# The last block of an eight-stage transformer kernel: which engine empties PSUM, and how many chunks VectorE may lie behind TensorE

## The chip, the cores and the metric

The kernel runs on one core of a Trainium2 chip. The metric is the device time of one execution in microseconds (us), before the change the median of 3 runs. The engines are called PE (TensorE), DVE (VectorE), ACT (ScalarE), POOL (GpSimd) and SP (the queue that issues DMAs).

## The reference

The input x is (4, 512, 256). Eight sublayers follow one another, each `x = x + f(layernorm(x))`: causal attention, a gated feed-forward with retrieved experts, attention over features, the feed-forward again, attention with rotary positions, and then the three that the last block of the kernel computes:

```python
def ffn(x):                              # used twice, before and after the scan, same weights
    h = silu(x @ w_gate) * (x @ w_up)    # 1024 hidden members
    keep the 2 largest magnitudes in each group of 4 members of h, zero the others
    return h @ w_down

def scan(x):
    ct = concat([x shifted by one position, x])
    xv = sigmoid(relu(ct @ W_act.T))     # pairs (re, im) of 128 complex channels
    mag = sqrt(re*re + im*im); m = cummax(mag over positions)
    re, im = re / m, im / m
    kv = cumulative complex product over the 512 positions
    r = sigmoid(relu(ct @ W_rec.T))
    return (kv @ W_val.T) * r**4

x = x + ffn(layernorm(x)); x = x + scan(layernorm(x)); x = x + ffn(layernorm(x))
```

## The kernel before

x stays in SBUF for the whole kernel, as 16 tiles of 128 positions by 256, four tiles (NT) to a batch element. The change touches one function, `feed_forward_and_scan` (from L1438), which computes the last three sublayers for all four batch elements. It has one instruction stream for each engine, and the order of the work is written out by hand.

A **pass** is one feed-forward of one batch element (512 positions): passes 0 to 3 are the first feed-forward of elements 0 to 3, passes 4 to 7 the second. A pass has 8 **chunks** of 128 hidden members (FC = 8), so there are 64 chunks. Every engine walks through the same **slots** n = 0, 1, 2, ... In slot n:

- PE does `chunk(n)`: 6 matmuls for the gate (L1618) and 6 for the up projection (L1624), each a product of high and low halves, into two PSUM banks that chunks n and n+1 use in turn. Then `down(n - 7)` (L1634), 8 records of an fp32 matmul into banks 4 and 5, where a pass sums up, and then the jobs of its list `pe_at[n]`.
- ACT does the silu of the gate's bank (L1724), then `magnitude(n - 1)` (L1712), the absolute value of the product before, then `act_at[n]`.
- DVE does `product(n)` (L1870), silu times the up bank, which it reads from PSUM. Four chunks (a quad) hold the four members of each group, and the quad before is selected in three parts in slots n with n % 4 = 0, 1, 2: comparisons (L1879), counts (L1885 to L1889), and h times the mask (L1894). Then `dve_at[n]`.
- POOL has no slot work of its own; it normalises rows (L1744) when told to, and at the start it makes the low halves of the weights (L1750).

Between engines, semaphores count: a product waits for silu and up, silu(n) for product(n - 2), `down` of a quad for its selection, the first `down` of a pass for the addition of the pass before to x (L1904, DVE, from PSUM), a pass's first chunk for the low halves of its rows (L1763, DVE, from PSUM).

The scan of element b is cut into jobs that start at slot `scan_from(b)` = 8(b+1) + 7, that is 15, 23, 31, 39, and are spread over 16 slots (s is its first): statistics on DVE and normalisation on POOL in s; row transposes in s+2 (L1565); the act gate in s+3 and s+4 (L1574, with tanh and square on ACT, L1674 and L1675); sum of squares s+5; root on ACT s+6 (L1679); running maximum and reciprocal s+6 (L1793, L1794); division and 7 levels s+7, s+8; 6 tree steps s+9, s+10 (each four operations, L1811 to L1815); fill s+11; the output matmul, which waits until the scan is filled, and its two DVE steps for each half in s+12 (L1593, L1840, L1843); statistics of the second feed-forward's rows s+13, their transposes and halves s+15. The gate `rec` (L1583) is in s+6 and s+8. Two scans overlap: s+8 of one is s of the next. Banks 6 and 7 are taken in turn by the jobs that need one (`Turns`, L1427); each bank is free again when the job's own reader has read it.

```python
            for n in range(SLOTS):
                p = (n - DOWN_LAG) // FC - 1
                if (n - DOWN_LAG) % FC == 0 and 0 <= p < PASSES:
                    add_to_x(p)
                if n < CHUNKS:
                    product(n)
                q, part = n // QUAD - 1, n % QUAD
                if 0 <= q < CHUNKS // QUAD and part < 3:
                    select(q, part)
                ...
                for job in dve_at[n]:
                    do(job)
```

## Time and profile before

| | us |
|---|---|
| median of 3 runs (1680.29, 1680.30, 1686.45) | 1680.3 |
| the profiled execution's own time | 1688.6 |
| its span, first to last instruction | 1686.8 |
| the last block's matmuls begin | 1229.5 |
| PE / DVE / ACT / POOL busy in the span | 1423.4 / 1078.2 / 617.3 / 286.1 |
| mean granted TensorE clock | 0.90 |

All times in the rows are counted from the first instruction of the profiled execution. Busy time is time in which an engine's unit works; instructions of DVE that follow one another overlap a little, so start-to-start distances are shorter than the durations. Matmul records of fp32 operands come in twos. A bracket such as `[5.40 <-ACT tail_silu L1724]` is the engine's idle time before the instruction and what ended it.

### The profile page before, as it was taken

Reading aid. Unit: us, or ns where it says so; the run is one execution under the profiler, and the core shown is the slowest. Engines: PE = TensorE matmul, PEld = TensorE weight load, DVE = VectorE, ACT = ScalarE, POOL = GpSimd, SP = SyncE. Lnnn points to the kernel's source line nnn. Section 1 sums busy time; section 2 is a strip of 40 time slices with the busy share of each in tenths; the row PEclk is TensorE's granted clock in tenths of the full one; section 3 lists DMA queues with packets and bytes.
Section 4 is the critical chain, followed back from the end, with each engine's and each line's share of the span. In section 5 each row is a group of like instructions: output and inputs, shape, how many; then the busy total and the mean of one; then the engine's idle time right before and its main releaser. Section 6 shows DMA issues by size and latency. Waiting matters only on the chain. (4 is left out here: it accounts for less than half of the span.)

```text
span 1686.8 us, 21695 instructions
## 1 busy us (share of the span) xinstructions
PE 1423.4 (84%) x8144; PEld 1010.8 (60%) x8144; DVE 1078.2 (64%) x2161; ACT 617.3 (37%) x1144; POOL 286.1 (17%) x239
## 2 busy tenths in 40 slices
PE   3899999858999678799957899988579977979698
PEld 2555555447888567688843334433268765766576
DVE  5555444087788348777647465566367688787875
ACT  1354444343333214333322465566422422333221
POOL 1210000053433102233323030200210101011000
PEclk9799987579999898899976599999979998989899
DMA  6713500040000000000022330300000000000000
GB/s 145 102 28 57 75 3 2 1 145 1 1 1 1 1 1 1 1 1 1 1 54 39 75 66 17 48 2 1 1 1 1 1 0 1 1 1 0 13 13 25
DMA packets 21407, 39.07 MB, mean 23 GB/s; under 512 B 4480, under 2 KB 6272, under 8 KB 21176
## 3 DMA queue, kind: packets, MB, share of 16 engines
q1 hardware_dynamic: 21304, 37.70, 11.9%
q8 instruction: 64, 1.05, 0.3%
q14 instruction: 39, 0.32, 0.1%
HBM read 14.54 MB, written 2.10 MB: 10 GB/s over the span
## 5 line engine op out<-in xcount | busy, mean ns | idle before, releaser
L1274 DVE TENSOR_REDUCE attn_negm<-ps 128x2 f32<-128x1024 f32 (+3 forms) x256 | 256.3, 1021 | 122.9 <-PE ps L903 61.2
L1123 ACT ACTIVATE attn_probs<-ps 128x512 f32<-128x512 f32 (+3 forms) x512 | 236.9, 515 | 211.1 <-PE ps L936 123.5
L453 POOL TENSOR_TENSOR moe_h_low<-moe_h,moe_h_high 128x512 fp32r<-128x512 f32 x96 | 139.7, 1458 | 326.9 <-ACT moe_h_high L403 326.9
L927 PE MATMUL ps<-attn_qs,attn_ks 49*128 49x512 f32 (+4 forms) x512 | 159.5, 437 | 36.6 <-ACT attn_probs L1123 34.5
L1634 PE MATMUL ps<-sb_f_down,tail_h 128*128 128x256 f32 x512 | 132.0, 406 | 56.7 <-DVE x L1904 41.1
L1634 PEld LDWEIGHTS ps<-sb_f_down,tail_h 128*128 128x128 f32 x512 | 102.5, 203 | 78.3 <-DVE x L1904 44.0
L903 PE MATMUL ps<-attn_ks,attn_qs 48*128 48x512 f32 (+4 forms) x512 | 126.4, 490 | 24.7 <-DMA attn_ks<-attn_part_low 18.2
L420 ACT ACTIVATE moe_silu<-ps 128x512 f32<-128x512 f32 x96 | 57.4, 598 | 228.7 <-PE ps L326 228.6
L927 PEld LDWEIGHTS ps<-attn_qs,attn_ks 51*128 51x128 f32 (+1 forms) x512 | 75.8, 204 | 100.9 <-ACT attn_probs L1123 96.1
L951 PE MATMUL ps<-attn_probs,attn_va 128*32 128x512 f32 (+3 forms) x1024 | 132.4, 595 | 0.0
L903 PEld LDWEIGHTS ps<-attn_ks,attn_qs 50*128 50x128 f32 (+1 forms) x512 | 54.4, 209 | 95.6 <-issue 63.8
L1870 DVE TENSOR_TENSOR tail_h<-tail_silu,ps 128x512 f32<-128x512 f32 x64 | 43.8, 686 | 84.5 <-PE ps L1624 45.1
L1724 ACT ACTIVATE tail_silu<-ps 128x512 f32<-128x512 f32 x64 | 38.1, 595 | 114.6 <-PE ps L1618 114.5
L476 DVE TENSOR_TENSOR moe_h<-moe_silu,ps 128x512 f32<-128x512 f32 x64 | 43.4, 687 | 55.2 <-PE ps L333 37.6
L355 PE MATMUL ps<-f_down_high,moe_h_high 128*128 128x256 f32 x256 | 74.3, 290 | 3.7 <-POOL moe_h_low L453 3.7
L355 PE MATMUL ps<-f_down_high,moe_h_low 128*128 128x256 f32 x256 | 72.8, 284 | 0.0
L355 PE MATMUL ps<-f_down_low,moe_h_high 128*128 128x256 f32 x256 | 72.4, 283 | 0.0
L403 ACT ACTIVATE moe_h_high<-moe_h 128x512 fp32r<-128x512 f32 x96 | 60.0, 625 | 27.0 <-DVE moe_h L476 26.4
L1239 DVE RECIPROCAL attn_rden<-ps 128x16 f32<-128x16 f32 x32 | 8.2, 258 | 95.5 <-PE ps L965 95.5
L1618 PE MATMUL ps<-tail_xh,tail_gate_high 128*128 128x512 f32 x128 | 63.0, 492 | 1.4 <-DVE tail_xl L1763 1.4
L1879 DVE TENSOR_TENSOR tail_ge<-tail_mag 128x1536 bf16<-128x1536 f32 (+2 forms) x48 | 55.8, 1219 | 0.7 <-ACT tail_mag L1712 0.7
L936 PE MATMUL ps<-sb_a_mask_kq,sb_identb 64*128 64x128 bf16 x512 | 55.6, 236 | 0.0
(316 smaller groups left out, 3287.1 us busy)
## 6 DMA issues: line engine op xcount, KB each, us to landing
attn_qs<-attn_part_high SPq DMA_DIRECT2D x64, 128.0 KB, 4.8
attn_qs<-attn_part_low SPq DMA_DIRECT2D x32, 128.0 KB, 4.5
attn_ks<-attn_part_high SPq DMA_DIRECT2D x32, 128.0 KB, 5.8
attn_ks<-attn_part_low SPq DMA_DIRECT2D x16, 128.0 KB, 6.6
out_x<-x SPq DMA_DIRECT2D x4, 512.0 KB, 2.8
x<-in_x SPq DMA_DIRECT2D x1, 1536.0 KB, 11.8
attn_qs<-attn_mT SPq DMA_DIRECT2D x64, 4.0 KB
moe_raw<-in_f_gate SPq DMA_DIRECT2D x2, 512.0 KB, 6.1
```

The lines of the kernel that those rows point to most:

```text
L355: last = pe.matmul(ps[:, bank + t // 2, (t % 2) * D:(t % 2 + 1) * D], hp[:, j % RING, t * P:(t + 1) * P], wp[:, jw, :], start=j == 0 and t ...
L403: act.activation(hc.high[:, n % RING, :], h[:, n % RING, :], ACT.Copy).then_inc(high_done, 1)
L420: act.activation(sg[:, j % 2, :], ps[:, 2 * (j % 2), :], ACT.Silu).then_inc(silu_done, 1)
L453: pool.tensor_tensor(hc.low[:, j % RING, :], h[:, j % RING, :], hc.high[:, j % RING, :], ALU.subtract).then_inc(low_done, 1)
L903: last = pe.matmul(ps[:, 2 * (n % 2) + k, 0:width1(qt)], qs[e:e + ROWS1, b % 2, hd // 2, qt * P:(qt + 1) * P], ks[e:e + ROWS1, b % 2, key_ ...
L927: last = pe.matmul(ps[:, SC + k, 0:width2(kt)], ks[e:e + ROWS2, b % 2, key_tile(hd), kt * P:(kt + 1) * P], qs[e:e + ROWS2, b % 2, hd // 2, ...
L951: last = pe.matmul(ps[SLOT * j:SLOT * (j + 1), CTX, T - width2(kt):T], va[:, b % 2, kt, hd % KH, :], pr[:, s3 % RING, j, 0:width2(kt)], st ...
L1123: act.activation(pr[:, s2 % RING, j, 0:n], ps[:, SC + k, 0:n], ACT.Exp, scale=HD ** -0.5).then_inc(exp_done, 1)
L1274: dve.tensor_reduce(m, ps[:, 2 * half:2 * half + 2, 0:width1(qt)], AX, ALU.max, negate=True).then_inc(r1_free, 1)
L1618: last = pe.matmul(ps[:, bank, :], wp[:, c, j * P:(j + 1) * P], xp[:, p % 2, c, :], start=c == 0 and k == 0, stop=c == DC - 1 and k == 2)
L1634: last = pe.matmul(ps[:, DOWN + t // 2, (t % 2) * D:(t % 2 + 1) * D], h[:, j, t * P:(t + 1) * P], w_down[:, j, :], start=j == 0 and t % 2 ...
L1879: c.do(dve.tensor_tensor(ge[:, first:first + n, :], mag[:, lo, :].unsqueeze(1).broadcast_to([P, n, T]), mag[:, lo + 1:4, :], ALU.is_ge))
```

## The change

All in `feed_forward_and_scan`:

- ACT copies the up bank to SBUF (`up`, a ring of 4), so `product` has both operands in SBUF; silu's ring grows from 2 to 4, h from 8 to 12 chunks, the magnitudes from one quad to two. ACT also copies the pass's sum (`dsum`), the scan's output (into `ta`), and the rows of a pass in fp32 (`xf`) beside their high halves. DVE reads no PSUM any more.
- `magnitude` is made 3 slots after its chunk instead of 1, and stands ahead of the up copy. The selection of a quad starts in slot 4q+5 instead of 4q+4, and `down` lies 10 slots behind instead of 7.
- The scan of element b starts at slot 8(b+2) (16, 24, 32, 40) instead of 8(b+1)+7, with its pieces at other distances: all levels and the division in one slot (s+8), the tree in one (s+9), the fill in s+10, DVE's output steps and the statistics after them in s+11, while PE's and ACT's part of the output stays in s+12.
- The low halves of rows are made by POOL in one instruction of 128x1024 for a pass; for pass 0 by DVE. POOL waits for the first normalised rows before it splits the weights.
- The addition to x is one instruction, in slot 8(p+2).

```diff
-    DOWN_LAG = 7
+    RING = 4
+    HRING = 3 * QUAD
+    ABS_LAG, SELECT_LAG, DOWN_LAG = 3, 5, 10
     SLOTS = CHUNKS + DOWN_LAG + 2
     DOWN = 4
     S1 = 8
@@ -1454,64 +1456,68 @@
     TREE = [1 << k for k in range((NS - 1).bit_length())]
 
     def scan_from(b):
-        return FC * (b + 1) + DOWN_LAG
+        return FC * (b + 2)
...
+    def rows_of(p, n):
+        pe_at[n] += [("row", "f", p, c) for c in range(DC)]
+        act_at[n] += [("row", "f", p, c) for c in range(DC)]
+        pool_at[n] += [("low", p)]
+
     for p in range(1, B):
-        pe_at[FC * p - 4] += [("row", "f", p, c) for c in range(DC)]
-        act_at[FC * p - 4] += [("row", "f", p, c) for c in range(DC)]
-        dve_at[FC * p - 4] += [("row", "f", p, c) for c in range(DC)]
-        pool_at[FC * p - 6].append(("normalise", "f", p))
+        pool_at[FC * p - 7].append(("normalise", "f", p))
+        rows_of(p, FC * p - 4)
     dve_at[0].append(("stats", "rest"))
+    for p in range(PASSES):
+        act_at[FC * (p + 1) - 1 + DOWN_LAG].append(("sum", p))
+        dve_at[FC * (p + 2)].append(("add", p))
     for b in range(B):
         s = scan_from(b)
         dve_at[s].append(("stats", "s", b))
-        pool_at[s].append(("normalise", "s", b))
-        pe_at[s + 2] += [("row", "s", b, c) for c in range(DC)]
-        act_at[s + 2] += [("row", "s", b, c) for c in range(DC)]
-        pe_at[s + 3].append(("act", b, 0))
-        pe_at[s + 4].append(("act", b, 1))
-        act_at[s + 3].append(("act", b, 0))
-        act_at[s + 4] += [("act", b, 1), ("square", b)]
+        pool_at[s + 2].append(("normalise", "s", b))
+        pe_at[s + 4] += [("row", "s", b, c) for c in range(DC)]
+        act_at[s + 4] += [("row", "s", b, c) for c in range(DC)]
+        pe_at[s + 5] += [("act", b, 0), ("act", b, 1)]
+        act_at[s + 5] += [("act", b, 0), ("act", b, 1), ("square", b)]
         dve_at[s + 5].append(("sum", b))
-        act_at[s + 6].append(("root", b))
-        dve_at[s + 6].append(("peak", b))
-        dve_at[s + 7] += [("divide", b)] + [("level", b, i) for i in (1, 2, 3)]
-        dve_at[s + 8] += [("level", b, i) for i in (4, 5, 6, 7)]
-        dve_at[s + 9] += [("tree", b, d) for d in TREE[:3]]
-        dve_at[s + 10] += [("tree", b, d) for d in TREE[3:]]
-        dve_at[s + 11].append(("fill", b))
-        pe_at[s + 6].append(("rec", b, 0))
-        act_at[s + 6].append(("rec", b, 0))
-        pe_at[s + 8].append(("rec", b, 1))
-        act_at[s + 8].append(("rec", b, 1))
+        pe_at[s + 7].append(("rec", b, 0))
+        act_at[s + 7].append(("rec", b, 0))
+        act_at[s + 8].append(("root", b))
+        dve_at[s + 7].append(("peak", b))
+        dve_at[s + 8] += [("divide", b)] + [("level", b, i) for i in range(1, S1)]
+        pe_at[s + 9].append(("rec", b, 1))
+        act_at[s + 9].append(("rec", b, 1))
+        dve_at[s + 9] += [("tree", b, d) for d in TREE]
+        dve_at[s + 10].append(("fill", b))
         pe_at[s + 12] += [("out", b, m) for m in range(2)]
-        dve_at[s + 12] += [("out", b, m) for m in range(2)]
-        dve_at[s + 13].append(("stats", "f", B + b))
-        pool_at[s + 13].append(("normalise", "f", B + b))
-        pe_at[s + 15] += [("row", "f", B + b, c) for c in range(DC)]
-        act_at[s + 15] += [("row", "f", B + b, c) for c in range(DC)]
-        dve_at[s + 15] += [("row", "f", B + b, c) for c in range(DC)]
+        act_at[s + 12] += [("out", b, m) for m in range(2)]
+        dve_at[s + 11] += [("out", b, m) for m in range(2)]
+        dve_at[s + 11].append(("stats", "f", B + b))
+        pool_at[s + 14].append(("normalise", "f", B + b))
+        rows_of(B + b, s + 15)
...
-            jobs.take(job, "dve" if job[0] == "out" or job[:2] == ("row", "f") else "act")
+            jobs.take(job, "act")
...
-        sg = s.sb("silu", [P, 2, T])
-        h = s.sb("h", [P, FC, T])
+        h = s.sb("h", [P, HRING, T])
-        mag = s.sb("mag", [P, QUAD, T])
+        mag = s.sb("mag", [P, 2, QUAD, T])
+        xf = s.sb("xf", [P, DC, T])
+        sg, up = s.sb("silu", [P, RING, T]), s.sb("up", [P, RING, T])
+        dsum = s.sb("dsum", [P, 2, T])
...
-                    pe.wait_ge(free["dve"], jobs.count[("row", "f", p, DC - 1)])
+                    pe.wait_ge(xl_ready, p + 1)
...
-                at_least(pe, prod_done, n - 1)
+                at_least(pe, up_done, n - 1)
...
-                    at_least(pe, x_done, p)
+                    at_least(pe, sum_done, p)
...
                 if kind == "f":
-                    act.activation(xT.high[:, k % 2, c, :], ps[:, jobs.bank[job], :], ACT.Copy).then_inc(xh_ready, 1)
+                    at_least(act, xl_ready, k)
+                    act.activation(xf[:, c, :], ps[:, jobs.bank[job], :], ACT.Copy).then_inc(xf_ready, 1)
+                    act.activation(xT.high[:, k % 2, c, :], ps[:, jobs.bank[job], :], ACT.Copy).then_inc(free["act"], 1)
...
+            def values(b, m):
+                job = ("out", b, m)
+                act.wait_ge(ready, jobs.number[job])
+                act.activation(ta[:, m, :], ps[:, jobs.bank[job], :], ACT.Copy).then_inc(free["act"], 1)
+
+            def down_sum(p):
+                act.wait_ge(down_done, FC * (p + 1))
+                at_least(act, x_done, p)
+                act.activation(dsum[:, :, :], ps[:, DOWN:DOWN + 2, :], ACT.Copy).then_inc(sum_done, 1)
...
             def magnitude(n):
                 act.wait_ge(prod_done, n + 1)
                 if n % QUAD == 0:
-                    at_least(act, ge_done, n // QUAD)
-                act.activation(mag[:, n % QUAD, :], h[:, n % FC, :], ACT.Abs).then_inc(mag_done, 1)
+                    at_least(act, ge_done, n // QUAD - 1)
+                act.activation(mag[:, n // QUAD % 2, n % QUAD, :], h[:, n % HRING, :], ACT.Abs).then_inc(mag_done, 1)
...
                 if n < CHUNKS:
                     act.wait_ge(gate_ready, n + 1)
-                    at_least(act, prod_done, n - 1)
-                    act.activation(sg[:, n % 2, :], ps[:, 2 * (n % 2), :], ACT.Silu).then_inc(silu_done, 1)
-                if 1 <= n <= CHUNKS:
-                    magnitude(n - 1)
+                    at_least(act, prod_done, n - RING + 1)
+                    act.activation(sg[:, n % RING, :], ps[:, 2 * (n % 2), :], ACT.Silu).then_inc(silu_done, 1)
+                if 0 <= n - ABS_LAG < CHUNKS:
+                    magnitude(n - ABS_LAG)
+                if n < CHUNKS:
+                    act.wait_ge(up_ready, n + 1)
+                    act.activation(up[:, n % RING, :], ps[:, 2 * (n % 2) + 1, :], ACT.Copy).then_inc(up_done, 1)
                 for job in act_at[n]:
                     do(job)
...
+            def low(p):
+                pool.wait_ge(xf_ready, DC * (p + 1))
+                pool.wait_ge(free["act"], jobs.count[("row", "f", p, DC - 1)])
+                pool.tensor_tensor(xT.low[:, p % 2, :, :], xf[:, :, :], xT.high[:, p % 2, :, :], ALU.subtract).then_inc(xl_ready, 1)
+
+            pool.wait_ge(xn_ready["f"], 1)
             for k, (n, at) in enumerate(parts):
                 pool.wait_ge(w_high, k + 1)
                 pool.tensor_tensor(halves[n].low[at], raw[n][at], halves[n].high[at], ALU.subtract).then_inc(w_low, 1)
             for n in range(SLOTS):
                 for job in pool_at[n]:
-                    normalise(*job[1:])
+                    if job[0] == "normalise":
+                        normalise(*job[1:])
+                    else:
+                        low(*job[1:])
 
         @block.vector
         def _(dve):
             c = Chain(dve, sel_steps, 11)
...
+            def low0():
+                dve.wait_ge(free["act"], jobs.count[("row", "f", 0, DC - 1)])
+                dve.tensor_tensor(xT.low[:, 0, :, :], xf[:, :, :], xT.high[:, 0, :, :], ALU.subtract).then_inc(xl_ready, 1)
...
-                dve.wait_ge(ready, jobs.number[job])
-                dve.tensor_tensor(r4[:, m, :], ps[:, jobs.bank[job], :], r4[:, m, :], ALU.mult).then_inc(free["dve"], 1)
-                dve.wait_ge(free["dve"], jobs.count[job])
+                dve.wait_ge(free["act"], jobs.count[job])
+                co.step(dve.tensor_tensor(r4[:, m, :], ta[:, m, :], r4[:, m, :], ALU.mult))
                 xb = x[:, NT * b + 2 * m:NT * b + 2 * m + 2, :]
                 dve.tensor_tensor(xb, xb, r4[:, m, :].rearrange("p (t d) -> p t d", t=2), ALU.add).then_inc(x_scanned, 1)
...
             def product(n):
-                dve.wait_ge(silu_done, n + 1)
-                dve.wait_ge(up_ready, n + 1)
-                at_least(dve, down_done, n - FC + 1)
-                dve.tensor_tensor(h[:, n % FC, :], sg[:, n % 2, :], ps[:, 2 * (n % 2) + 1, :], ALU.mult).then_inc(prod_done, 1)
+                dve.wait_ge(up_done, n + 1)
+                at_least(dve, down_done, n - HRING + 1)
+                dve.tensor_tensor(h[:, n % HRING, :], sg[:, n % RING, :], up[:, n % RING, :], ALU.mult).then_inc(prod_done, 1)
...
             def add_to_x(p):
-                dve.wait_ge(down_done, FC * (p + 1))
-                for k in range(2):
-                    t0 = NT * (p % B) + 2 * k
-                    xk = x[:, t0:t0 + 2, :]
-                    last = dve.tensor_tensor(xk, xk, ps[:, DOWN + k, :].rearrange("p (t d) -> p t d", t=2), ALU.add)
-                last.then_inc(x_done, 1)
+                dve.wait_ge(sum_done, p + 1)
+                xb = x[:, NT * (p % B):NT * (p % B + 1), :]
+                dve.tensor_tensor(xb, xb, dsum[:, :, :].rearrange("p k (t d) -> p (k t) d", t=2), ALU.add).then_inc(x_done, 1)
...
-            for job in early:
-                do(job)
+            low0()
             for n in range(SLOTS):
-                p = (n - DOWN_LAG) // FC - 1
-                if (n - DOWN_LAG) % FC == 0 and 0 <= p < PASSES:
-                    add_to_x(p)
                 if n < CHUNKS:
                     product(n)
-                q, part = n // QUAD - 1, n % QUAD
+                q, part = (n - SELECT_LAG) // QUAD, (n - SELECT_LAG) % QUAD
                 if 0 <= q < CHUNKS // QUAD and part < 3:
                     select(q, part)
                 if n == FC:
```

## Rows read from the trace of the kernel before

**Rows 1.** Windows: us, busy us (instructions) by engine, granted clock (PEclk), DMA share, GB/s.

```profile
1229.45:1264.30 34.85, 29.59 (x113) 23.63 (x113) 21.89 (x58) 10.36 (x18) 7.18 (x8) 0.84 0.00 1
1264.30:1302.75 38.45, 38.12 (x170) 31.84 (x169) 25.68 (x39) 10.14 (x18) 0.00 (x0) 0.97 0.00 1
1433.89:1505.52 71.63, 57.75 (x243) 45.11 (x241) 59.03 (x141) 22.29 (x32) 6.57 (x8) 0.93 0.00 1
1498.00:1502.00 4.00, 3.58 (x9) 2.86 (x10) 3.83 (x13) 0.00 (x0) 0.00 (x0) 0.50 0.00 0
```

**Rows 2.** Waits, last block: who waited for whom, us, times, longest.

```profile
PE ps L1634 <- DVE x L1904: 41.1, 7, 11.1
```

**Rows 3.** Timeline, DVE: start, us, line, operation, [idle before <- releaser].

```profile
1388.05 0.69 DVE L1870 TENSOR_TENSOR tail_h<-tail_silu,ps 128x512 f32<-128x512 f32 x1 [0.25 <-DVE tail_zz L1815]
...
1438.76 0.69 DVE L1870 TENSOR_TENSOR tail_h<-tail_silu,ps 128x512 f32<-128x512 f32 x1 [2.26 <-PE ps L1634]
1439.37 3.49 DVE L1879 TENSOR_TENSOR tail_ge<-tail_mag 128x1536 bf16<-128x1536 f32 x3
...
1447.21 0.69 DVE L1885 TENSOR_TENSOR tail_count<-tail_ge 128x1024 bf16<-128x1024 bf16 x1
...
1453.43 2.49 DVE L1894 SCALAR_TENSOR_TENSOR tail_h<-tail_count,tail_h 128x512 f32<-128x512 bf16 x4
...
1459.57 0.69 DVE L1870 TENSOR_TENSOR tail_h<-tail_silu,ps 128x512 f32<-128x512 f32 x1 [0.25 <-DVE tail_zz L1815]
...
1470.07 0.69 DVE L1870 TENSOR_TENSOR tail_h<-tail_silu,ps 128x512 f32<-128x512 f32 x1 [5.40 <-ACT tail_silu L1724]
...
1474.38 1.40 DVE L174 BATCH_NORM_STATS2 tail_nf_stats<-x 128x6 f32<-128x256 f32 x4 [0.21 <-DVE tail_ge L1879]
...
1478.80 0.68 DVE L1787 TENSOR_TENSOR tail_sq<-tail_sq 128x512 f32<-128x512 f32 x1
```

**Rows 4.** Chain that ended last, scan round of 1531: start, us, what.

```profile
1531.19 3.69 PE ps L1593 x16
1534.88 3.44 PE ps L1574 x8
1538.32 1.38 PE ps L1618 x6
...
1541.06 1.73 PE ps L1634 x8
```

**Rows 5.** Timeline, PE: three starts after idle time.

```profile
1261.08 3.78 PE L1634 MATMUL ps<-sb_f_down,tail_h 128*128 128x256 f32 x8 [2.96 <-DVEq L1897]
...
1599.37 3.78 PE L1634 MATMUL ps<-sb_f_down,tail_h 128*128 128x256 f32 x8 [5.68 <-DVEq L1897]
1602.94 4.61 PE L1593 MATMUL ps<-sb_s_val,tail_zz 128*128 128x256 f32 x16
```

**Rows 6.** Timeline, ACT, same pass as rows 3.

```profile
1468.40 1.15 ACT L1675 ACTIVATE tail_sq<-tail_z,tail_halfone 128x1024 f32<-128x1024 f32 x1
...
1474.96 1.28 ACT L1679 ACT_TABLE_LOAD   x1
```

**Rows 7.** Timeline, POOL: two normalisations of four tiles.

```profile
1436.60 2.16 POOL L1744 TENSOR_SCALAR tail_xns<-x,tail_minus_s,tail_ns_rstd 128x256 f32<-128x256 f32 x4 [24.77 <-DVE tail_minus_s L1783]
1478.99 4.41 POOL L1744 TENSOR_SCALAR tail_xnf<-x,tail_minus_f,tail_nf_rstd 128x256 f32<-128x256 f32 x4 [40.23 <-DVE tail_minus_f L1783]
```

**Rows 8.** Timeline, POOL and DVE, start of the last block.

```profile
1220.61 2.34 POOL L1750 TENSOR_TENSOR tail_up_low<-sb_f_up,tail_up_high 128x1024 fp32r<-128x1024 f32 x1
1220.71 2.25 DVE L183 TENSOR_TENSOR tail_n_newton<-tail_n_rstd 128x4 f32<-128x4 f32 x1
...
1240.06 0.17 DVE L180 TENSOR_SCALAR tail_n_half<-tail_n_var 128x12 int32<-128x12 int32 x1
```

**Rows 9.** Groups of instructions, last block: busy us, mean ns, idle before.

```profile
L1840 DVE TENSOR_TENSOR tail_r<-ps,tail_r 128x512 f32<-128x512 f32 x8 | 5.5, 692 | 7.3 <-PE ps L1593 7.3
L1843 DVE TENSOR_TENSOR x<-x,tail_r 128x512 f32<-128x512 f32 x8 | 5.5, 691 | 0.3
```

More of the change, by code:

```diff
@@ L1698, in do @@
                     row(*a)
+                elif kind == "sum":
+                    down_sum(*a)
+                elif kind == "out":
+                    values(*a)
                 elif kind == "act":
@@ L1798, in divide @@
                 if b > 0:
-                    dve.wait_ge(ready, jobs.number[("out", b - 1, 1)])
+                    dve.wait_ge(free["act"], jobs.count[("out", b - 1, 1)])
                 dve.scalar_tensor_tensor(zz[:, :, :], z[:, :, :], 1.0, sq[:, 1, :].unsqueeze(1).broadcast_to([P, 2, T]),
@@ L1846, in do @@
                 kind, *a = job
-                if kind == "row":
-                    row(*a)
+                if kind == "add":
+                    add_to_x(*a)
                 elif kind == "stats":
```

20 lines of the change are left out of this document (8 added, 12 removed).

## The prediction

> **What bounds the kernel now.** I read the windows by pass first, then who waited for whom, then one pass instruction by instruction. The change touches only the last block, whose PE work starts at 1229.45 us [rows 1]. Call F the moment when VectorE (DVE) has signalled that a scan is filled; the four of them fall at 1387.9, 1459.4, 1531.1 and 1602.8 us [rows 3 to 5], so one pass with a scan in it takes 71.6 us. A plain pass (slots 8 to 15) takes 38.5 us and TensorE (PE) is busy for 38.1 of them: PE bounds it. In a pass with a scan PE is busy 57.8 of 71.6 us and DVE 59.0 [rows 1]. DVE issues nearly all the time: the waits of that pass longer than 0.2 us add up to 9.7 (2.3, 1.3, 0.2, 5.4, 0.3, 0.2; the two long ones stand in [rows 3]), so 61.9 us is its own work with the small gaps between dependent steps. PE in turn loses 41.1 us in seven waits for the addition to x [rows 2]. So a scan pass is a loop through all engines: DVE's work plus what DVE waits for.
>
> **The change, part by part.** The profiled execution spans 1686.8 us (1688.6 with what lies around it) against a median of 1680.3; I work in the span and carry the difference over.
>
> *Operands from SBUF.* The 64 products and the scan's outputs lose their PSUM operand. An addition that read PSUM took 692 ns and one that read SBUF alone 691 [rows 9]: zero gain by instruction. The Trainium skill (VectorE: DVE Perf Modes, section on the TRN2 errata) gives 58 cycles plus the elements for an SBUF source against 120 for PSUM; by that some 11 instructions a pass would each save 65 ns, an estimate of 5 us in the block. The rows show none of it.
>
> *Work taken from DVE.* The two lows of rows (xl, 0.69 each as any 128x512 operation here) go to GpSimd (POOL), and two additions to x become one: 61.9 - 1.4 leaves 60.5 us of DVE per scan pass. If nothing else waited, that would be the pass. ACT gains 8 copies of 0.6, a copy of the sum and two more copies of rows, some 8 us on an engine busy for 22 of 71.6: hidden, except where a copy stands in a hand-off.
>
> *The start.* POOL now waits for the first normalised rows before it splits the weights. Today its four 2.34 us subtractions hold up four tiny DVE steps (2.25 us each but the first, 1.5, where such a step else takes 0.17) [rows 8]: 7.5 us for the four. The rows come at 1218.5, but two weight subtractions must now follow (1223.2), then DVE's low beside POOL, so chunk 0 starts at 1224.6, 4.9 earlier. Then the longer lags: today chunk 8 starts 34.9 us after chunk 0 (at 1264.3), because slot 7 already holds a down product that waits for the selection. Later it is 8 chunks of 2.72, rows of 0.8 and 1.7 for a cold start, 24.3: chunk 8 at 1249.0. Slots 8 and 9 are chunk alone, slots 10 to 15 chunk and down (2.75 + 1.72 = 4.5) [rows 4]: chunk 16 at 1282.1 instead of 1302.8. Of these 20.7 us, 5.2 are three down products that only come later. The first scan now starts at slot 16, not 15, and its sum waits for ACT's slot 17, so DVE has the statistics at 1298 and the first scan's act gates end at 1318.7 on PE. From there it goes as in the next paragraph, 2.4 us shorter, as no rows cross there: first F at 1374.5, **13.4 earlier**.
>
> *A scan pass, from F (t = 0).* With s the slot in which a scan starts, PE stands at the scan's output of slot s+4 and has idled for about 18 us. After an idle of 11 us the granted clock was 0.50 for 4 us [rows 1], the level of 1.2 GHz. After one of 5.7 us, 8 records of down took 3.8 us instead of 1.7 and the 16 of the output 4.6 instead of 3.7 [rows 4, 5]; I call that cold. So the output takes 5.6, ACT's copy 0.75, DVE's last two steps 1.4: out ends at 7.8, the statistics (4.4, [rows 3]) at 12.2, two products at 13.4. The comparison of slot s+5 needs the magnitude of chunk s+3, which ACT makes in slot s+6, behind the act gates. PE: output 5.6, rows 1.3 (its banks wait for ACT), chunk and down 4.5, both act parts 6.4 (3.2 each, 3.44 with the end of the last matmul [rows 4]) = 17.8. ACT: relu 0.8, tanh and square 2.2 (the square 1.15 [rows 6]), silu and magnitude 1.2 = 22.0. **DVE stalls 8.6 us.** Then comparison 3.6, sum 0.6, product 0.6, counts 2.65, product 0.6, selection 2.6 [rows 3] = 32.7. The peak of slot s+7 needs the root of ACT's slot s+8, behind chunk s+8: PE 17.8 + 8.9 + 0.8 = 27.5, ACT's four copies 2.2, POOL's subtraction 2.9, chunk and its copy 3.7, table load 1.3 [rows 6], root 0.65 = 38.1. **DVE stalls 5.4 more.** What is left of the 60.5 (less the 22.4 already spent) is 38.1, with no wait in it: the next F at 76.2, **4.6 later than today's 71.6**. That holds for two rounds. In the third no new scan starts, which saves its statistics (4.4): 71.8 against 71.7. The moved scan pieces cost nothing by themselves; where they land decides, and both waits are of an earlier DVE slot on a later ACT slot.
>
> *POOL's subtraction.* No row has it. The nearest, 128x1024 of weights, takes 2.34 [rows 8]; POOL's normalisation took 2.16 alone and 4.41 beside DVE [rows 7]. Ends: 2.35 and 4.8. I take 2.9, nearer the lower one, because DVE is about to stall then. The rows also show DVE standing through a POOL instruction. The Trainium skill (SBUF — State Buffer, section "SBUF: two separate sides") says the port pair is an exclusive lock held for the whole instruction, against a GpSimd operation also for a DVE operation with two SBUF inputs, as the products now are. The trace agrees, and that speaks against this edit; rival B has its price.
>
> *The end.* From the last F: chunk 56 waits in the same way for rows, copies and subtraction and starts at 24.8, PE idle for 4.6 before it and so cold (1.9). Chunk 63 starts 31.3 later, at 58.0; its last 2.75 and three downs 5.2 give 66.0; sum, copy and addition 2.6, comparison to selection 9.0, four downs 7.2, copy and addition 2.6, store and rest 3.5 = 90.9. Today 84.0 passes from the last F to the end: **6.9 later**.
>
> Sum: -13.4 + 4.6 + 4.6 + 0.1 + 6.9 = **+2.8 us**, or 1683 at the median. A measurement of this kernel can tell about 0.5% (8.4 us) from no change: below 1671.9 is faster, above 1688.7 slower.
>
> **Rivals.**
> A, the lags do what they say: DVE works through the scans with at most one of the two stalls. Without the stall at the root each of three rounds loses 5.4: 1683 - 16 = 1667; without both, 1641. For it: POOL and ACT are idle for most of the time, and the lags are written for this. Against it: both waits follow from the slot numbers. It decides if the root is through by t = 35. Chance 0.18.
> B, slower: the hand-off at the end of a pass. Rows, four copies and one subtraction now lie in a row before the next chunk. If POOL takes 4.8 beside DVE instead of 2.9, PE idles over 3 us there, and after idles of 3.0 and 5.7 us the next 8 records took 3.8 us [rows 5]. That is 1.9 + 1.3 at three boundaries and 1.9 at the last: +11.5, 1694. It decides from 1.5 us more per boundary. Chance 0.20.
> C, several small waits that I left out, each under 0.3 us, in some 60 slots: +7 to +12, 1690 to 1695. Chance 0.07.
> D, the start gains nothing, since the weights are only split later: +5 to +13, 1688 to 1696. Against it: the 3 us wait before the first down goes in any case. Chance 0.03.
>
> **How the numbers follow.** My forecast (within 5 us of 1683) has 0.52. All of it and part of A's mild end and of B fall within 0.5%: same 0.55. Slower takes most of B, C and D: 0.26; faster most of A: 0.19. The bounds: subtraction at 2.35 (-2), PE not cold at the output (-2 in each round, -6), subtraction at 4.8 (+8), cold boundaries (+4). With A's 1667 and B's 1694 the range is 1667 to 1695; it leaves out A without any stall and the worst of B and C.
>
> **What would show it.** Right: chunk 16 starts near 1282 and the first F at 1374 to 1376; in each scan round DVE waits some 8 us for a magnitude and some 5 for the root; the distance between two F is 76; the clock is at half when the output starts; the last F is at 1598 to 1600. Wrong: a distance below 71, PE busy when the scan is filled, or a comparison that doesn't wait; on the other side POOL's subtraction above 4 us, or PE idle for more than 3 us at the boundary. If chunk 0 isn't earlier than 1227, the start is misjudged.

## The result and the profile after

The changed kernel takes **1696.4 us**, the median of 20 runs (1685.6 to 1716.6). The kernel before takes 1684.4 in 20 runs beside them (1676.9 to 1699.7); the 1680.3 of the table above was the median of its first three. The ratio is **1.0067, with a 95% interval of 1.0044 to 1.009**: slower by some 11 us. The middle of the interval lies above the 0.5% that the prediction named as the least it could tell, its lower end just below. The ratio leaves out runs more than 1.5% above the fastest of their kernel (two of after), the medians don't.

| us | before | after | forecast |
|---|---|---|---|
| median | 1684.4 | 1696.4 | 1683 (1667 to 1695) |
| profiled execution: own time / span | 1688.6 / 1686.8 | 1686.7 / 1684.7 | |
| its mean granted clock | 0.902 | 0.905 | |
| last block, from its first instruction | 474.2 | 488.6 | 477.0 |

The profiled execution of after is one of the quickest of its 20, and its span is even shorter than that of before. So the spans can't be compared, and the windows show it. Windows, first of before, then of after (columns as in [rows 1]): the attention stage, which the change doesn't touch, and the last block.

```profile
856.60:1212.50 355.90, 299.47 (x1472) 136.32 (x1472) 197.94 (x258) 176.36 (x338) 48.31 (x47) 0.87 0.20 36
1212.50:1686.80 474.30, 388.39 (x1632) 310.71 (x1632) 354.35 (x760) 135.79 (x205) 49.54 (x48) 0.92 0.01 5
```

```profile
850.60:1196.00 345.40, 287.60 (x1472) 131.54 (x1472) 197.74 (x258) 176.32 (x338) 48.45 (x47) 0.91 0.20 37
1196.00:1684.70 488.70, 389.30 (x1632) 312.87 (x1632) 349.18 (x737) 190.79 (x301) 81.55 (x55) 0.89 0.01 5
```

The same 1472 matmuls took 10.5 us less at a granted clock of 0.91 than at 0.87: a difference between two executions, not of the change. The block took 14.4 us more with the same 1632 matmuls. ACT gains 55.0 us of work and POOL 32.0, as was meant; DVE loses only 5.2. From here on I compare blocks, cut at the same instructions in each trace. F0 to F3 are the products that follow the fills.

| us | chunk 0 starts | 0 to 8 | 8 to 16 | 16 to F0 | F0-F1, F1-F2, F2-F3 | F3 to end (chunk 56, 63 start after F3) |
|---|---|---|---|---|---|---|
| before | 16.9 | 34.9 | 38.5 | 85.3 | 71.5, 71.7, 71.7 | 83.9 (27.2, 58.4) |
| after | 11.7 | 29.4 | 32.9 | 93.5 | 78.0, 76.5, 72.5 | 94.3 (26.9, 60.3) |
| forecast | 12.0 | 24.3 | 33.1 | 92.4 | 76.2, 76.2, 71.8 | 90.9 (24.8, 58.0) |

So up to F0 the change gains 8.1 us (forecast 13.4), the rounds lose 12.1 (9.3), and the end loses 10.4 (6.9).

**A round.** Timeline of DVE in after, start, us, line and operation, with the idle time before it; F1 is at 1441.41. It answers to [rows 3].

```profile
1441.41 0.69 DVE L1902 TENSOR_TENSOR tail_h<-tail_silu,tail_up 128x512 f32<-128x512 f32 x1 [0.21 <-DVE tail_zz L1848]
1442.02 2.49 DVE L1926 SCALAR_TENSOR_TENSOR tail_h<-tail_count,tail_h 128x512 f32<-128x512 bf16 x4
...
1463.37 3.50 DVE L1911 TENSOR_TENSOR tail_ge<-tail_mag 128x1536 bf16<-128x1536 f32 x3 [8.75 <-ACT tail_mag L1735]
...
1471.48 4.64 DVE L1926 SCALAR_TENSOR_TENSOR tail_h<-tail_count,tail_h 128x512 f32<-128x512 bf16 x4
1479.46 1.23 DVE L1826 TENSOR_TENSOR_SCAN tail_sq<-tail_sq 128x512 f32<-128x512 f32 x1 [3.33 <-ACT tail_sq L1688]
```

Both stalls of the forecast are there: the comparison waits 8.75 us for a magnitude (forecast 8.6), the scan of the peak 3.33 for the root (5.4). The selection between them takes 4.64 instead of 2.5, beside POOL's subtraction, so both stalls with it are 14.2 us where the forecast had 14.0. What feeds the first stall is seen on PE and ACT (timelines of the same kernel; PE's answers to [rows 5]):

```profile
1441.40 5.32 PE L1600 MATMUL ps<-sb_s_val,tail_zz 128*128 128x256 f32 x16 [18.06 <-DVEq L1865]
1447.41 0.66 PE L1572 MATMUL ps<-sb_ident,tail_xns 128*128 128x128 f32 x4 [0.25 <-ACT tail_ta L1707]
...
1450.67 1.89 PE L1641 MATMUL ps<-sb_f_down,tail_h 128*128 128x256 f32 x8
1452.39 7.03 PE L1581 MATMUL ps<-tail_xs,sb_s_act 128*128 128x512 f32 x16
```

```profile
1461.19 1.15 ACT L1684 ACTIVATE tail_sq<-tail_z,tail_halfone 128x1024 f32<-128x1024 f32 x1
1462.24 0.58 ACT L1747 ACTIVATE tail_silu<-ps 128x512 f32<-128x512 f32 x1
1462.72 0.62 ACT L1735 ACTIVATE tail_mag<-tail_h 128x512 f32<-128x512 f32 x1
```

PE had idled 18.06 us when the fill came (forecast "about 18"). Then output, rows, chunk, down and act gates run before ACT can make the square, silu and the magnitude. The windows of the same kernel for the round, for PE's first 3.8 us after the fill and for the 18 us before it:

```profile
1441.41:1517.93 76.52, 57.36 (x241) 44.98 (x241) 59.97 (x137) 29.62 (x45) 11.76 (x9) 0.88 0.00 1
1441.40:1445.20 3.80, 3.80 (x10) 3.12 (x11) 3.10 (x5) 0.17 (x1) 0.00 (x0) 0.56 0.00 0
1423.40:1441.40 18.00, 0.00 (x0) 0.03 (x1) 17.14 (x38) 1.11 (x2) 5.99 (x4) 0.62 0.00 0
```

The granted clock was 0.56, close to the level of 1.2 GHz, in the first 3.8 us. In the 18 us DVE was busy for 17.1, and PE for none: the rows, a chunk and a down stood behind the output in PE's queue, though they don't need the fill (e3).

The output did not always take 5.3 us. The first and the third round of after, timeline of PE:

```profile
1363.42 6.75 PE L1600 MATMUL ps<-sb_s_val,tail_zz 128*128 128x256 f32 x16 [18.04 <-DVEq L1865]
...
1517.92 6.30 PE L1600 MATMUL ps<-sb_s_val,tail_zz 128*128 128x256 f32 x16 [18.06 <-DVEq L1865]
```

After the same 18 us without work, the same 16 records took 6.75, 5.32 and 6.30 us. The granted clock was 0.50, the level of 1.2 GHz, for their first 6.2, 3.3 and 5.3 us. In the kernel before each of the three took 3.69 (one is in [rows 4]), at a granted clock of 1.00 (1459.50 to 1463.00). So of the 12.1 us that the three rounds lose, the outputs' lengths are 7.3 (18.4 in sum against 11.1) and all else is 4.8.

**The normalisations.** Timelines of POOL, then of PE, in after, at the start of the block, ahead of the first scan and at the end (those of POOL answer to [rows 7, 8]):

```profile
1206.52 3.35 POOL L1782 TENSOR_TENSOR tail_gate_low<-sb_f_gate,tail_gate_high 128x1024 fp32r<-128x1024 f32 x1
...
1222.11 4.13 POOL L1770 TENSOR_SCALAR tail_xnf<-x,tail_minus_rest,tail_n_rstd 128x256 f32<-128x256 f32 x4 [9.91 <-DVE tail_minus_rest L1804]
...
1286.21 8.03 POOL L1770 TENSOR_SCALAR tail_xns<-x,tail_minus_s,tail_ns_rstd 128x256 f32<-128x256 f32 x4 [22.52 <-DVE tail_minus_s L1816]
...
1603.06 8.57 POOL L1770 TENSOR_SCALAR tail_xnf<-x,tail_minus_f,tail_nf_rstd 128x256 f32<-128x256 f32 x4 [51.77 <-DVE tail_minus_f L1816]
```

```profile
1226.38 1.94 PE L1572 MATMUL ps<-sb_ident,tail_xnf 128*128 128x128 f32 x8 [2.49 <-POOL tail_xnf L1770]
...
1611.77 1.78 PE L1572 MATMUL ps<-sb_ident,tail_xnf 128*128 128x128 f32 x8 [2.08 <-POOL tail_xnf L1770]
...
1617.34 0.80 PE L1625 MATMUL ps<-tail_xh,tail_gate_high 128*128 128x512 f32 x1 [3.79 <-POOL tail_xl L1777]
```

The same normalisation of four tiles took 2.16 and 4.41 in [rows 7], and takes 4.13, 8.03 and 8.57 here, where DVE runs products, comparisons and counts at the same time. The eleven on POOL take 2.16 to 5.27 us in before and 2.60 to 8.57 in after. What speaks for the operands is the same place in the kernel before, the normalisation of pass 1, which took 2.16 beside two products that read PSUM (timeline of DVE and POOL in before, then of DVE in after):

```profile
1242.40 1.29 DVE L1870 TENSOR_TENSOR tail_h<-tail_silu,ps 128x512 f32<-128x512 f32 x2
1242.59 2.16 POOL L1744 TENSOR_SCALAR tail_xnf<-x,tail_minus_rest,tail_n_rstd 128x256 f32<-128x256 f32 x4 [19.65 <-DVE tail_minus_rest L1771]
```

```profile
1221.92 1.89 DVE L1902 TENSOR_TENSOR tail_h<-tail_silu,tail_up 128x512 f32<-128x512 f32 x3
```

Beside three products from SBUF (1.89 us) it takes 4.13, longer by 1.97. PE then waits 2.49 us for it and starts again slowly: 1.94 us for the rows where e5 has 1.03.

At 1603 the 8.57 us lie ahead of chunk 56.

**The end.** Chain that ended last, in after: start, us, what.

```profile
1660.10 1.23 DVE x L1934
1661.33 3.41 DVE tail_ge L1911 x3
...
1670.15 8.78 PE ps L1641 x32
```

The addition of pass 6, which nothing at the end needs yet, stands ahead of the last comparison. The last four downs take 8.8 us instead of 7.2, after 2.85 us of idleness. Those 2.85 us alone don't decide it. Timeline of PE in e5, the same four downs:

```profile
1675.92 7.17 PE L1645 MATMUL ps<-sb_f_down,tail_h 128*128 128x256 f32 x32 [2.85 <-DVEq L1939]
```

In e5 and e8 they take 7.17 after the same 2.85 us, in the other five runs below with that wait (e1 to e4, e7) 8.7 to 10.2.

### The profile page after: what moved, and what is told of

It reads as the page before. It is cut to its first block and busy times, and to the rows that moved or that the text cites. A ratio compares the mean times of both kernels' runs of the same rounds, so it can differ in the third digit from the quotient of the medians.

```text
span 1684.7 us, 21764 instructions
## 1 busy us (share of the span) xinstructions
PE 1408.8 (84%) x8144; PEld 1005.1 (60%) x8144; DVE 1067.3 (63%) x2138; ACT 672.1 (40%) x1240; POOL 327.0 (19%) x246
## 5 line engine op out<-in xcount | busy, mean ns | idle before, releaser
L927 PE MATMUL ps<-attn_qs,attn_ks 49*128 49x512 f32 (+4 forms) x512 | 156.1, 423 | 38.3 <-ACT attn_probs L1123 35.6
L903 PE MATMUL ps<-attn_ks,attn_qs 48*128 48x512 f32 (+4 forms) x512 | 122.1, 474 | 24.3 <-DMA attn_ks<-attn_part_low 17.8
L951 PE MATMUL ps<-attn_probs,attn_va 128*32 128x512 f32 (+3 forms) x1024 | 127.1, 573 | 0.0
L1641 PE MATMUL ps<-sb_f_down,tail_h 128*128 128x256 f32 x512 | 121.3, 383 | 4.0 <-DVEq L1929 2.9
L1641 PEld LDWEIGHTS ps<-sb_f_down,tail_h 128*128 128x128 f32 x512 | 97.9, 192 | 20.0 <-DVEq L1929 3.3
L1600 PE MATMUL ps<-sb_s_val,tail_zz 128*128 128x256 f32 x64 | 24.3, 562 | 67.1 <-DVEq L1865 67.1
L403 ACT ACTIVATE moe_h_high<-moe_h 128x512 fp32r<-128x512 f32 x96 | 59.9, 624 | 18.2 <-DVE moe_h L476 17.7
L1902 DVE TENSOR_TENSOR tail_h<-tail_silu,tail_up 128x512 f32<-128x512 f32 x64 | 44.6, 707 | 33.0 <-ACT tail_up L1752 29.1
```

What stands on the lines that cost most here:

```text
L403: act.activation(hc.high[:, n % RING, :], h[:, n % RING, :], ACT.Copy).then_inc(high_done, 1)
L903: last = pe.matmul(ps[:, 2 * (n % 2) + k, 0:width1(qt)], qs[e:e + ROWS1, b % 2, hd // 2, qt * P:(qt + 1) * P], ks[e:e + ROWS1, b % 2, key_ ...
L927: last = pe.matmul(ps[:, SC + k, 0:width2(kt)], ks[e:e + ROWS2, b % 2, key_tile(hd), kt * P:(kt + 1) * P], qs[e:e + ROWS2, b % 2, hd // 2, ...
L951: last = pe.matmul(ps[SLOT * j:SLOT * (j + 1), CTX, T - width2(kt):T], va[:, b % 2, kt, hd % KH, :], pr[:, s3 % RING, j, 0:width2(kt)], st ...
L1641: last = pe.matmul(ps[:, DOWN + t // 2, (t % 2) * D:(t % 2 + 1) * D], h[:, m % HRING, t * P:(t + 1) * P], w_down[:, j, :], start=j == 0 an ...
```

## The experiments

Each takes the changed kernel, but for the one that says otherwise. Where no number of runs is given, it is one. A profiled run's whole time moves with the clock (e2 and e5 had means of 0.892 and 0.899), so the block is given with it.

The rounds vary by themselves: two runs that touch nothing in them (e5, e11) have 225.5 and 224.9 us in sum, against 227.0 in after. What varies is the length of the output. Less its three outputs, the sum is the same within 0.2 us:

| us, three rounds | before | after | e5 | e11 | e1 | e2 | e3 | e4 | e7 | e8 |
|---|---|---|---|---|---|---|---|---|---|---|
| sum | 214.9 | 227.0 | 225.5 | 224.9 | 224.3 | 216.9 | 208.0 | 200.8 | 220.3 | 229.3 |
| of it the three outputs | 11.1 | 18.4 | 17.0 | 16.5 | 17.4 | 18.0 | 16.5 | 18.9 | 10.9 | 16.0 |
| the rest | 203.8 | 208.6 | 208.4 | 208.5 | 206.9 | 198.9 | 191.5 | 182.0 | 209.4 | 213.3 |

**e1_root_early.** The root is made an ACT slot earlier.

```diff
-        act_at[s + 7].append(("rec", b, 0))
-        act_at[s + 8].append(("root", b))
+        act_at[s + 7] += [("root", b), ("rec", b, 0)]
```

> The root of the scan moves from ACT's slot s+8 (behind chunk s+8) to slot s+7, ahead of rec. The loop theory: DVE's wait of 3.3 us for the root goes, but in the same slot s+8 the addition to x then waits for ACT's copy of the sum, which ends 1484.1 in the second scan round of the changed kernel, so a round shortens by only 0.5 to 1 us, from 76.5 to about 75.8 between two fills. The rival that each wait stands for itself: 76.5 to 73.2, 13 us over four scans.

Measured 1683.2 us, block 485.2, rounds 76.0, 77.2, 71.1. Timeline of DVE in e1:

```profile
1470.08 4.65 DVE L1925 SCALAR_TENSOR_TENSOR tail_h<-tail_count,tail_h 128x512 f32<-128x512 bf16 x4
1474.87 1.22 DVE L1825 TENSOR_TENSOR_SCAN tail_sq<-tail_sq 128x512 f32<-128x512 f32 x1
...
1482.76 1.23 DVE L1933 TENSOR_TENSOR x<-x,tail_dsum 128x1024 f32<-128x1024 f32 x1 [2.55 <-ACT tail_dsum L1711]
```

The scan waits no longer, and the addition to x behind it now waits 2.55 us for ACT's copy of the sum. The rounds' sum falls by 2.7 us, and by 1.7 without the outputs, 0.6 a round. The wait for the root was real, but it stood in front of another one.

**e2_root_add.** That one too: the addition of pass b moves behind the division and the levels, to the end of the same slot.

```diff
-        dve_at[FC * (p + 2)].append(("add", p))
...
-        dve_at[s].append(("stats", "s", b))
+        dve_at[s] += [("add", b), ("stats", "s", b)]
...
+    for p in range(B, PASSES):
+        dve_at[FC * (p + 2)].append(("add", p))
```

> Root early as in the run before, and the addition to x behind the division and the levels of the same slot. The loop theory: now nothing waits there, DVE's 3.3 us go: 76.5 to 73.2 between two fills. The rival that POOL's hold on the port sets the pace (subtraction beside the selection, which took 4.6 instead of 2.5): no change beyond 1 us, since DVE is held anyway.

Measured 1696.3 us at a clock of 0.892, block 476.0: 12.6 less than after. From chunk 16 to F0 it is 3.0 shorter, and the rounds (74.7, 73.2, 69.0) give up 10.1 in sum, without the outputs 9.7, 3.2 each. So the two waits together, for the root and for the sum, are worth what the scan alone was seen to wait, 3.3 us, and the root's alone didn't give it.

**e3_out_late.** PE's and ACT's part of the output lies one slot later, so that PE makes the rows of the scan and a chunk before it waits for the fill. DVE's order is as it was.

```diff
-        pe_at[s + 12] += [("out", b, m) for m in range(2)]
-        act_at[s + 12] += [("out", b, m) for m in range(2)]
+        pe_at[s + 13] += [("out", b, m) for m in range(2)]
+        act_at[s + 13] += [("out", b, m) for m in range(2)]
```

> The scan's output matmul and ACT's copies of it move from slot s+12 to s+13, so that PE does the rows of the next scan, chunk s+13 and its down before the scan is filled, in the 18 us in which it is idle now. The loop theory (PE's work behind the fill lies on the path up to the magnitude): the act gates end 5.9 us earlier, DVE's wait of 8.8 us for the magnitude falls to about 3, and a round goes from 76.5 to about 70.8. The rival that DVE alone bounds the round (60 us of work and POOL's hold): the wait moves to the root, less than 2 us gained.

Measured 1675.1 us, block 470.4 (18.2 less), rounds 70.6, 70.9, 66.5. Timelines of e3, DVE and PE:

```profile
1457.10 3.50 DVE L1911 TENSOR_TENSOR tail_ge<-tail_mag 128x1536 bf16<-128x1536 f32 x3 [2.93 <-ACT tail_mag L1735]
...
1473.21 1.23 DVE L1826 TENSOR_TENSOR_SCAN tail_sq<-tail_sq 128x512 f32<-128x512 f32 x1 [3.34 <-ACT tail_sq L1688]
```

```profile
1429.24 1.94 PE L1572 MATMUL ps<-sb_ident,tail_xns 128*128 128x128 f32 x8 [6.47 <-POOL tail_xns L1770]
...
1440.90 5.38 PE L1600 MATMUL ps<-sb_s_val,tail_zz 128*128 128x256 f32 x16 [3.59 <-DVEq L1865]
```

The wait for the magnitude falls from 8.75 to 2.93, by 5.8: that is the rows' 1.3 and the 4.5 of a chunk and a down, which now run in idle time ahead of the fill. The rest of the round is unchanged, the 3.34 us for the root too. That is the price of the loop's first stall, shown by shortening it, and the largest of the change. The rounds fall by 6.3 us each, and by 5.7 without the outputs. The output itself stays cold here: 5.38 us after 3.59 us of idleness.

**e4_three.** Both edits of e2 and that of e3.

> Root early, addition behind the levels, and output a slot later, together. The loop theory: a round of 67 to 69 us between two fills, against 76.5 in the changed kernel and 71.6 in the kernel before; the last block 25 to 30 us shorter than in the changed kernel, and the kernel some 12 to 18 us (0.7 to 1.1%) faster than before. The rival that other waits take their place: within 0.5% of the kernel before.

Measured in five rounds of runs: 1669.9 us (12 runs) against 1681.7 of before (17), ratio **0.9904 (0.987 to 0.9938)**. Block 460.7, rounds 69.0, 68.5, 63.4. The two savings add up: without the lengths of the four outputs, e2's block is 12.0 us shorter, e3's 15.7 and e4's 27.6. With both stalls repaired the longer lags beat the kernel before.

**e5_norm_dve.** DVE makes the normalisations of passes 1 and 7, as it makes that of pass 0; four tiles take it 1.38 us.

```diff
-        pool_at[FC * p - 7].append(("normalise", "f", p))
+        if p > 1:
+            pool_at[FC * p - 7].append(("normalise", "f", p))
...
+    dve_at[0] += [("stats", "rest"), ("norm", 1)]
...
+            if b < B - 1:
+                pool_at[s + 14].append(("normalise", "f", B + b))
+            else:
+                dve_at[s + 11].append(("norm", B + b))
...
+            def norm_rows(p):
+                dve.wait_ge(ready, jobs.number[("row", "f", p - 1, DC - 1)])
+                norm_apply(dve, x, p % B, nb_rest if p < B else nb["f"], xn["f"]).then_inc(xn_ready["f"], 1)
```

> In the changed kernel, the normalisations of passes 1 and 7 on DVE instead of POOL (4.1 and 8.6 us beside DVE's own work). If POOL's turn at the memory port costs what I left out: chunk 8 follows chunk 0 by 25 us instead of 29.4, and the end from the last fill is 90 instead of 94.3, the block 8 to 9 us shorter. If TensorE and the other lags set these stretches: no more than 2 us in all.

Measured 1690.6 us at a clock of 0.899, block 477.8 (10.8 less). Chunk 8 starts 25.1 us after chunk 0 instead of 29.4 (forecast of the prediction: 24.3), and chunk 56 at F3 + 24.3 instead of 26.9 (24.8). With POOL out of these two hand-offs both lie within 0.8 us of where the prediction had put them. Of the 10.8, these two are 6.9. The end is 89.2 long instead of 94.3: beside the 2.6 ahead of chunk 56, the last four downs took 7.17 instead of 8.76, which nothing ties to the edit. The rounds' 1.5 are their outputs'. DVE makes four tiles in 1.38 us where POOL took 2.16 undisturbed, so this run prices the hand-off through POOL as it was, not the stretching alone.

**e7_warm.** Before PE waits for the fill, it waits for a product that DVE makes shortly before and runs 16 matmuls into the output's bank; their result is overwritten by the output.

```diff
+                if m == 0:
+                    pe.wait_ge(prod_done, scan_from(b) + 11)
+                    for k in range(16):
+                        pe.matmul(bank, w_gate.high[:, 0, 0:P], xT.high[:, 0, 0, :], start=True, stop=True)
                 pe.wait_ge(filled, b + 1)
```

> In the changed kernel, 16 matmuls into the bank of the scan's output, whose result is overwritten, from the moment DVE enters the slot of the fill, so that TensorE is busy for some 5.5 us until just before the fill. If the lower clock after 18 us of idle time costs the path: the output's 16 records fall from 5.3 to 3.7 us and each round by 1.6 to 1.8, four times, about 7 us in the block. If the output's time is hidden behind DVE: under 1 us in the block.

Measured 1688.5 us, block 480.3 (8.3 less), rounds 75.1, 75.1, 70.1. Groups of instructions (busy us, mean ns of one, idle before), of after and of e7:

```profile
L1600 PE MATMUL ps<-sb_s_val,tail_zz 128*128 128x256 f32 x64 | 24.3, 562 | 67.1 <-DVEq L1865 67.1
```

```profile
L1604 PE MATMUL ps<-sb_s_val,tail_zz 128*128 128x256 f32 x64 | 14.6, 381 | 0.3 <-DVEq L1869 0.3
```

The outputs' 64 matmuls are busy for 9.7 us less, 2.4 for each output: in the three rounds 3.1, 1.7 and 2.7, and the rounds follow with 2.9, 1.4 and 2.4. Now the first two rounds are equal: the scatter is gone with the cold outputs. The prediction had put 2 us a round on a cold output in its bounds.

**e8_low_dve.** The low half of rows is made by DVE in one instruction instead of POOL, so no POOL instruction lies in the hand-off at a pass's end.

```diff
-        pool_at[n] += [("low", p)]
+        dve_at[n] += [("low", p)]
```

> In the changed kernel, the lows of rows back on DVE (one 128x1024 instruction a pass from SBUF) instead of POOL. The loop theory: DVE has waits on both sides of this place, so 1.3 us more work and a selection not held up by POOL (2.5 instead of 4.6 us) leave a scan round at 76.5 within 1 us. The rival that POOL's subtraction at the end of the pass costs the round (my rival B): 3 us or more less in each round.

Measured 1694.5 us, block 487.9, rounds 77.8, 78.3, 73.2. Without the outputs they are 4.7 us longer in sum, 1.6 each; the expected "within 1 us of 76.5" is missed by 0.8 in the second round. Timeline of DVE in e8:

```profile
1480.22 2.49 DVE L1928 SCALAR_TENSOR_TENSOR tail_h<-tail_count,tail_h 128x512 f32<-128x512 bf16 x4
1482.86 1.23 DVE L1797 TENSOR_TENSOR tail_xl<-tail_xf,tail_xh 128x1024 fp32r<-128x1024 f32 x1
```

The selection is back at 2.49 us, and the scan then waits 5.70 for the root instead of 3.33. Beside POOL's subtraction the selection takes 2.2 us more in each round, and these are paid out of a stall. The subtraction itself stands in the path to the root, as forecast: POOL's ended 32.4 us after F1 in after, DVE's, behind the selection, ends at 34.0 here, and the scan of the peak starts 1.7 us later (39.7 instead of 38.1). **Rival B falls** as the price of a round: on POOL the subtraction took 2.7 in the rounds, not 4.8. The end is 3.1 us shorter: 1.6 of it are the last four downs at 7.17 us, 0.8 lie ahead of chunk 56, no more than in e11 (0.9), which leaves the subtraction where it was, and 0.7 between chunks 56 and 63.

**e9_before_start.** The kernel before, with POOL's wait alone.

```diff
+            pool.wait_ge(xn_ready["f"], 1)
             for k, (n, at) in enumerate(parts):
```

> The kernel before with one line of the change: POOL waits for the first normalised rows before it splits the weights. If that line alone gives the earlier start: chunk 0 comes 11.5 to 12 us after the block's start instead of 16.9, and as the rest is as before, the block is 5 us shorter (474.2 to 469). The rival that the weights' split then delays chunk 0: within 1 us of 16.9.

Measured 1672.4 us, block 467.1 instead of 474.2. Timeline of DVE in e9, one of the steps that took 2.25 us in [rows 8]:

```profile
1206.18 0.16 DVE L183 TENSOR_TENSOR tail_n_newton<-tail_n_rstd 128x4 f32<-128x4 f32 x1
```

Chunk 0 starts at 10.7 us of the block instead of 16.9. One line of the change, alone, is worth 7.1 us in the block, 6.2 of it ahead of chunk 0. The single run doesn't resolve that in the whole time. So the start's gain is not one of the lags or of the SBUF operands: measured from this kernel, everything else in the change costs 21.5 us (467.1 to 488.6), and of the repaired kernels e3 (470.4) is still behind it, e4 (460.7) ahead by 6.4.

**e11_end.** ACT's copy of pass 6's sum goes one slot later and its addition four DVE slots later, behind the last selection.

```diff
-        act_at[FC * (p + 1) - 1 + DOWN_LAG].append(("sum", p))
-        dve_at[FC * (p + 2)].append(("add", p))
+        act_at[FC * (p + 1) - 1 + DOWN_LAG + (p == PASSES - 2)].append(("sum", p))
+        dve_at[FC * (p + 2) + 4 * (p == PASSES - 2)].append(("add", p))
```

> The changed kernel with only the end altered: ACT copies the sum of pass 6 one slot later, behind the last magnitude, and DVE adds it behind the last selection. If the order at the end costs what the walk said (the last comparison stands behind an addition that waits for a down product three slots late): from chunk 63 to the end 30 us instead of 33.9. If PE's eight last down products set the end alone: within 0.5 us of 33.9.

Measured 1686.2 us, block 482.4. From chunk 63 to the end 30.5 us instead of 33.9. Timeline of PE in e11:

```profile
1671.33 7.17 PE L1641 MATMUL ps<-sb_f_down,tail_h 128*128 128x256 f32 x32 [1.02 <-DVEq L1929]
```

Idle 1.02 instead of 2.85 before the last four downs, and these 7.17 instead of 8.76: 3.4 us together. The 1.8 of idleness are the edit's. The 1.6 came in e5 and e8 without it, so they are not shown to be. The block's other 2.9 us lie in rounds (2.0) and ahead of chunk 56 (0.9), which the edit leaves alone.

**e10_all.** e4, e5 and e11 together.

> The changed kernel with everything that paid alone: root early, addition behind the levels, output a slot later, normalisations of passes 1 and 7 on DVE, and at the end the sum of pass 6 behind the last magnitude with its addition behind the last selection. If the parts add up: the block 445 to 450 us (474.2 before, 488.6 with the change), the kernel about 1.5% faster than before. The rival that gains in PE's path are given back at DVE: 455 or more.

Measured in five rounds of runs: 1653.7 us (6 runs) against 1680.6 (11), ratio **0.9852 (0.9804 to 0.9899)**. Block 441.3, 47.3 less than after where the three parts alone make 45.0, and somewhat below the 445 to 450 expected.

**e12_all_warm.** e10 and the extra matmuls of e7.

> As e10_all, with the 16 matmuls that keep TensorE busy before the scan is filled. If the lower clock still costs the path there: 1.5 to 2 us less in each scan round than e10_all, the block 5 to 7 us shorter. The rival that with the output a slot later the path has slack: within 1.5 us of e10_all.

Measured in five rounds: 1646.6 us (1624.9 to 1657.3), ratio **0.975 (0.9678 to 0.9821)**. Three of its six runs count in that ratio; the medians of all give 0.980. Block 434.9, 6.4 less than e10, and its four outputs are 6.4 shorter (14.8 against 21.2). This version beats both kernels, the one before by 2.0 to 2.5%. Against e10 the medians differ by 7.1 us, but their ranges overlap; what shows the gain is the block.

## Why the prediction was wrong

The sign (a few us slower) was right, the size wasn't: 12.1 us between the medians where 2.8 were forecast, and 1696.4 lies 1.4 above the range. 4.1 us of the distance to 1683 is the base: three runs of before gave 1680.3, twenty gave 1684.4. The rest is 9.3 us between the medians, and 11.6 between the two profiled blocks (14.4 against 2.8), which can be divided.

The step that failed is a term that the sum lacks: POOL's normalisation of the next rows, in the hand-off to TensorE at the start and at the end of the block, was put at nothing. It took 4.13 and 8.57 us beside VectorE, and without it there 6.9 us went (e5). Smaller parts are the length of the outputs and the last downs.

- **"The start ... 24.3: chunk 8 at 1249.0"** is the largest: 29.4, so **5.1 us** too little. The sum had eight chunks at a stretch and no term for the normalisation of pass 1. With both operands in SBUF, DVE's three waiting products stretched it from 2.16 to 4.13 us, then came 2.49 us of waiting on PE and a cold start. e5 shows that the hand-off through POOL was it (25.1). The prediction had both prices in [rows 7] and used the higher one only for the subtraction. Chunk 0 itself was right (11.7 against 12.0), and 16 to F0 was 1.1 short.
- **"The next F at 76.2"** held in kind: 78.0, 76.5 and 72.5, together **2.8 us** over. Both stalls are there. The first is right to 0.2 us (8.75 against 8.6), and e3 shortens it by the very work that the forecast had put in front of it; the second is 3.33 instead of 5.4, since the selection before it was stretched from 2.5 to 4.6, which e8 shows to be one and the same time. Together they are as forecast (14.2 against 14.0); the prediction's terms up to the root add up to 38.25, not 38.1, and the scan started at 38.05. The cold output was taken as 5.6 and took 6.75, 5.32 and 6.30: 1.6 of the 2.8. The other 1.2 lie in the first two rounds, 0.6 in each, and have no single place that I could find.
- **"The end ... 90.9"** was **3.4 us** short in two places. Chunk 56 starts at F3 + 26.9, not 24.8: the normalisation beside comparisons and counts took 8.57 (e5: 24.3). And the last four downs were counted warm (7.2) and took 8.8. They did so after 2.85 us of idleness, but took 7.17 after the same idleness in e5 and e8, so what decides it stays open.
- **POOL's subtraction** was taken as 2.9; the seven took 2.6 in the mean. It stands in the path to the root as forecast, and its price was right (e8). The bounds of 2.35 and 4.8 were put on this instruction, and none on the one that was stretched. That is what the range lacked: the two normalisations are 6.9 of the 11.6 us (e5).
- **Operands from SBUF**: the forecast gave nothing, and nothing came: the 64 products took 686 ns in the mean with the up bank in PSUM and take 707 from SBUF (median 687 and 692). The Trainium skill (VectorE: DVE Perf Modes, the section on the TRN2 errata) lists 58 cycles for an SBUF source and 120 for PSUM, from which the prediction estimated 65 ns a piece; the runs don't show them. The same section of the Trainium skill says that its 58 is too low and that an fp32 addition of 512 elements measured 691 ns; [rows 9] have 691. What did come with two SBUF operands is POOL held up by DVE: 4.13 to 8.57 us for four tiles that took 2.16 beside products from PSUM. The prediction cites the exclusive lock of the port pair (the Trainium skill, SBUF — State Buffer, "SBUF: two separate sides"), and the trace agrees. I had used it for DVE held by POOL, and it also works the other way.

Rival A (the lags do what they say) fails for the reason given: at the root and at the magnitude an earlier DVE slot waits for a later ACT slot. Only with both moved (e4) do the lags pay, measured from the kernel with e9's line. Rivals B, C and D had sizes near the result (1694, 1690 to 1695, 1688 to 1696), and none its mechanism: B by e8, D since chunk 0 came 5.2 us earlier in its block, C since 6.9 us of the miss sit in two hand-offs (e5).

## What to carry to other kernels

A lag in slots between two engines is only worth what the next in-order queue lets through: after each long-awaited result, list what every engine still has to run before the waiter's operand exists, and put whatever doesn't need the result ahead of the wait (here 5.7 us a round by one slot). When a wait is taken away, look for the one right behind it before counting a gain. An instruction moved or left on GpSimd must be priced beside the VectorE work that will run with it, above all where it stands in a hand-off that TensorE waits for, and then TensorE's cold start can come on top. And ask of each line of a change what it gives alone: here one line gave the whole gain at the start (e9), and hid what the rest cost.
